# The fourteen middle images written out one by one, in place of a loop with registers

## The reference

```python
# layer 0: attention over rows of each channel
Q, K, V = (_conv1x1(x, W, b).reshape(b * cr, m, n) for W, b in ...)
attn = softmax(einsum('gik,gjk->gij', Q, K), axis=-1)
y = _conv1x1(einsum('gij,gjn->gin', attn, V), Wr, br)
x = batch_norm(y) + x
# layer 1: 8 heads of attention over 1024 tokens, 32 channels a head
q, k, v = split(einsum('oc,bct->bot', w_qkv, group_norm(x)) + b_qkv)
weight = softmax(einsum('bct,bcs->bts', q * scale, k * scale))
x = x + einsum('oc,bct->bot', w_proj, einsum('bts,bcs->bct', weight, v)) + b_proj
# layer 2: linear attention with softmax over channels and over tokens
xn = group_norm(x); k, v = split(conv(xn)); q = softmax(k, axis=1) * q_scale
out = gelu(group_norm(einsum('bde,bdn->ben', einsum('bdn,ben->bde', softmax(k, 2), v), q)))
x = xn + einsum('bchw,oc->bohw', out, out_w) + out_b
# layer 3: 12-tap upsampling by 2 both ways, leaky relu, 12-tap downsampling by 2
x = down(leaky_relu(up(x + bias), 0.2) * sqrt(2))
```

## Time and profile before

| what | value |
|---|---|
| median of 3 runs | 3870.22 us (3865.36 to 3873.83) |
| the profiled execution, its own time | 3865.28 us |
| its span (first to last instruction) | 3863.4 us |
| granted TensorE clock, mean of the span | 0.957 |
| instructions recorded | 72651 |

### The profile page before, as it was taken

One profiled execution on the slowest core, in us unless ns is written; L12 is line 12 of the kernel. 1 busy time (PEld: TensorE's weight loads), 2 busy tenths in 40 slices (PEclk: granted clock), 3 DMA queues, 4 the chain that ended last, 5 costly groups with the idle time before them and its releaser, 6 DMA issues.

```text
span 3863.4 us, 72651 instructions
## 1 busy us (share of the span) xinstructions
PE 3622.2 (94%) x22401; PEld 1790.8 (46%) x22401; DVE 2890.1 (75%) x5019; ACT 2972.7 (77%) x6992; POOL 41.3 (1%) x57
## 2 busy tenths in 40 slices
PE   6989999999999999999999999999999999999987
PEld 3444545354453544545354453544545354453423
DVE  4667778778777777778778787777778778787755
ACT  2888878878787887878878787887878878788852
POOL 0000000000000000000000000000000000000000
PEclk7889999999999999999999999999999999999998
DMA  2212120121211112120121211112120121211100
GB/s 76 58 39 61 40 70 7 51 59 39 72 35 37 45 42 67 40 70 7 50 59 40 72 30 42 45 42 67 40 70 7 51 59 40 72 30 41 34 17 11
DMA packets 75657, 177.20 MB, mean 46 GB/s; under 512 B 16352, under 2 KB 19040, under 8 KB 73184
## 3 DMA queue, kind: packets, MB, share of 16 engines
q1 hardware_dynamic: 74656, 170.38, 16.2%
q10 hardware_dynamic: 576, 1.57, 0.2%
HBM read 36.62 MB, written 17.30 MB: 14 GB/s over the span
## 4 chain that ended last, share of the span: by engine, by line
PE 80%; issue 7%; DVE 7%; ACT 6%; SPq 0%; ACTq 0%; DMA 0%; DVEq 0%; POOL 0%; POOLq 0%
PE ps L1102 29%; PE ps L1167 12%; PE ps L1130 12%; PE ps L1146 10%; PE ps L1718 3%; ACT ps L986 3%; PE ps L1768 2%; DVE mxh L680 2%; PE ps L1653 2%; PE ps L1750 2%; PE ps L1760 2%; PE ps L1665 2%; PE ps L1777 2%; DVE k L819 1%; ACT u L1048 1%
## 5 line engine op out<-in xcount | busy, mean ns | idle before, releaser
L986 ACT ACTIVATE ps<-ps,mxh 128x512 f32<-128x512 f32 x2048 | 1365.8, 674 | 196.3 <-DVE mxh L680 169.2
L680 DVE TENSOR_REDUCE mxh<-ps 128x1 f32<-128x512 f32 x2048 | 1309.9, 679 | 273.9 <-PE ps L1146 266.1
L977 ACT ACTIVATE prob<-ps 128x512 f32<-128x512 f32 x2048 | 1122.0, 611 | 354.2 <-PE ps L1130 347.3
L1130 PE MATMUL ps<-qs,ks 97*128 97x512 f32 x2048 | 892.6, 513 | 38.3 <-issue 29.1
L1146 PE MATMUL ps<-ks,qs 96*128 96x512 f32 x2048 | 703.1, 419 | 33.3 <-ACT ps L986 18.3
L1130 PEld LDWEIGHTS ps<-qs,ks 97*128 97x128 f32 x2048 | 353.9, 195 | 603.9 <-issue 356.2
L1167 PE MATMUL ps<-prob,vo 128*32 128x512 f32 x4096 | 580.2, 640 | 0.0
L1146 PEld LDWEIGHTS ps<-ks,qs 96*128 96x128 f32 x2048 | 404.1, 197 | 179.9 <-ACT ps L986 79.2
L986 ACT ACTIVATION_READ_ACCUMULATOR ps<-ps,mxh 128x1 f32 x2048 | 443.2, 216 | 0.0
L1102 PE MATMUL ps<-xn,wqk 128*128 128x512 f32 x512 | 246.1, 614 | 13.3 <-DVE lo L663 9.3
L1102 PE MATMUL ps<-wkv,xn 128*128 128x512 f32 x512 | 244.5, 607 | 3.7 <-DVE xn L607 3.7
(11 more groups left out here) (121 smaller groups left out, 3576.8 us busy)
## 6 DMA issues: line engine op xcount, KB each, us to landing
qs<-hi SPq DMA_DIRECT2D x256, 128.0 KB, 2.3
ks<-hi SPq DMA_DIRECT2D x248, 128.0 KB, 2.3
xb<-in_x SPq DMA_DIRECT2D x32, 512.0 KB, 4.3
qs<-lo SPq DMA_DIRECT2D x128, 128.0 KB, 2.3
xa<-xb SPq DMA_DIRECT2D x16, 1024.0 KB, 4.6
recs<-recd SPq DMA_DIRECT2D x64, 256.0 KB
out<-xn SPq DMA_DIRECT2D x32, 512.0 KB, 2.6
ks<-lo SPq DMA_DIRECT2D x124, 128.0 KB, 2.3
```

The lines of the kernel that those rows point to most:

```text
L680: dve.tensor_reduce(mxh[:, k, e:e + 1], ps[:, MAX_BANKS[at % 3], :], AX_X, ALU.max, negate=True).then_inc(max_ok.sem, 1)
L977: act.activation(prob[:, n % 2, h, :], ps[:, k % 2, :], ACT.Exp).then_inc(p_ok.sem, 1)
L986: act.activation(ps[:, bank, :], ps[:, bank, :], ACT.Exp, bias=mxh[:, k, e:e + 1], accum_out=sumh[:, m // NT % 2, k, e:e + 1]).then_inc(su ...
L1130: pe.matmul(ps[:, k % 2, :], ks[0:STACK + 1, (u // 2) * Q4 + h, s * P:(s + 1) * P], qs[0:STACK + 1, u, h, :], start=True, stop=True).then_ ...
```

## The change

The loop of images 1 to 14 becomes a Python loop: the same period is written out 14 times, each time with plain numbers for b, i and j. The counter, the copies of the register, the register sums ahead of waits and the 13 jumps back (with the one that falls through) are gone; every wait is for a constant. Images 0 and 15, `first()` and `last()` are as they were. Each engine has the same instructions that work on data, in the same order. The kernel gets some 20 lines shorter, so that a line L1130 of before is L1109 of after.

```diff
     def __call__(self, image, k):
-        image, away = image if isinstance(image, tuple) else (image, 0)
-        return image * (self.per_image * self.size) + ((away * self.per_image + k) * self.size + START)
+        return (image * self.per_image + k) * self.size + START
...
-        def periods(eng, first, period, last):
+        def periods(first, period, last):
 
             first()
             period(0, None, 1)
-            with eng.Fori(1, B - 1) as b:
-                period((b, 0), (b, -1), (b, 1))
-            period(B - 1, B - 2, None)
+            for b in range(1, B):
+                period(b, b - 1, b + 1 if b < B - 1 else None)
             last(B - 1)
-
-        def copied(eng, n, *images):
-
-
-            if n % 4 or not isinstance(images[0], tuple):
-                return images
-            register = eng.alloc_register(f"image_at_step{n}")
-            eng.reg_mov(register, images[0][0])
-            copy = eng.snap(register, min_val=1, max_val=B - 2)
-            return [(copy, away) for _, away in images]
...
             def period(b, i, j):
                 for n in range(STEPS):
-                    b, i, j = copied(pe, n, b, i, j)
                     for pair in range(2):
                         logits(b, n, pair, i)
...
-            periods(pe, first, period, last)
+            periods(first, period, last)
```

More of the change, by code:

```diff
@@ L127, in __call__ @@
     def __call__(self, image, k):
-        image, away = image if isinstance(image, tuple) else (image, 0)
-        return image * (self.per_image * self.size) + ((away * self.per_image + k) * self.size + START)
-def number(image):
-    return image[0] + image[1] if isinstance(image, tuple) else image
+        return (image * self.per_image + k) * self.size + START
 def chain_kernel(nc, x, weights, vectors, rows, filters, consts, recd, out):
@@ L379, in load @@
                 for ct in range(CT):
-                    sp.dma_start(xb[:, ct, :], x[number(j), ct * P:(ct + 1) * P, :]).then_inc(x_in.sem, 16)
+                    sp.dma_start(xb[:, ct, :], x[j, ct * P:(ct + 1) * P, :]).then_inc(x_in.sem, 16)
             def copy_x(b, i, j):
@@ L429, in store @@
                 sp.wait_ge(o3_ok.sem, o3_ok(i, ct + 1))
-                sp.dma_start(out[number(i), ct * P:(ct + 1) * P, :], o3[:, ct, :]).then_inc(stored.sem, 16)
+                sp.dma_start(out[i, ct * P:(ct + 1) * P, :], o3[:, ct, :]).then_inc(stored.sem, 16)
             def side(name, b, i, j):
@@ L464, in period @@
                 for n in range(STEPS):
-                    b, i, j = copied(sp, n, b, i, j)
                     for name in [*beside(2 * n, i, j), *beside(2 * n + 1, i, j)]:
@@ L471, in last @@
                     side(name, None, i, None)
-            periods(sp, first, period, last)
+            periods(first, period, last)
             sp.wait_ge(stored.sem, stored(B, 0))
@@ L505, in period @@
                 for n in range(STEPS):
-                    b, i, j = copied(pool, n, b, i, j)
                     for name in [*beside(2 * n, i, j), *beside(2 * n + 1, i, j)]:
@@ L512, in last @@
                     side(name, None, i, None)
-            periods(pool, first, period, last)
+            periods(first, period, last)
         @block.vector
@@ L936, in period @@
                 for n in range(STEPS):
-                    b, i, j = copied(dve, n, b, i, j)
                     t = turn_at(n)
@@ L958, in last @@
                     side(name, None, i, None)
-            periods(dve, first, period, last)
+            periods(first, period, last)
         @block.scalar
@@ L1073, in period @@
                 for n in range(STEPS):
-                    b, i, j = copied(act, n, b, i, j)
                     for pair in range(2):
@@ L1090, in last @@
                     side(name, None, i, None)
-            periods(act, first, period, last)
+            periods(first, period, last)
         @block.tensor
```

## The result

| | median, us | runs |
|---|---|---|
| before | 3871.27 | 3865.36 to 3873.83 (4) |
| after | 3782.20 | 3780.32 to 3792.89 (4) |

The ratio is 0.9778, with a 95% interval of 0.9756 to 0.9799. The change gains 89 us; the forecast was 44.5, a time of 3824 us with a range from 3806 to 3843. The direction and the jumps came out as forecast. The other half of the gain stands in a term that the prediction had set at 1.4 us.

The account below looks back on a forecast made before the run. PE, busy 94% of the span, was taken as the bound. Jumps 43.1 plus registers 1.4 made 44.5 us less: 3820.8 from the profiled execution, 3825.7 from the median; 3824 us was set between, range 3806 to 3843.

Parts of the forecast that it names:

- The jumps: At the image boundaries: removing 13 jumps gains 43.1 us, about 26 of PE idle time and 17 of half-clock spells.
- The register instructions: Throughout the loop's images, ahead of waits: removing them gains 0.1 us an image, 1.4 us in all.
- the pair that I could measure (0): Line 1115 to line 1155, in the loop and in image 15 with constants: 20.90 us each, no difference.
- Its upper end: Most that removing register instructions could gain: 25 us, if 48 fused operations an image on PE each cost 37 ns.
- register instructions cost more: Rival: in an image's second half they stand between hand-overs of DVE, ACT and PE; up to 25 us, 3800 us; chance 7%.
- the slow clock stays: Rival: at the boundaries the idle time goes but half-clock spells remain; 27 us gained, 3841 us; chance 9%.
- Stalls of new code: Rival: engines stall on written-out instructions not yet fetched; 3925 us if PE is caught twice an image; chance 4%.
- the gap as cover: Rival: PE's 2 us idle at the jump let DVE and ACT catch up, so PE waits later; 3862 us; chance 3%.
- The instruction packets: Instruction fetch: the loop's body is already fetched each turn, 425 packets; written out, fewer register instructions to fetch, costed at nothing.
- The signs named: Profile after: no 3.4 us branch, boundaries 26.9 us at clock 1.00, PE busy some 17 us less, period 228.6 us.

Follow-up runs that it names:

- e1: Against before: the 14 periods written out without jumps, every register instruction kept on all engines; 3819.39 us, ratio 0.9873.
- e5: Against before: loop and registers kept, a prefetch hint added on the loop's back edge; 3826.33 us, ratio 0.9892.
- e9: The kernel after the change, unchanged, in a second round with a second profile; 3785.23 us, ratio 0.9773.
- e6: Against e1: register waits kept on PE alone, constants in the waits of all other engines; 3795.20 us, ratio 0.9808.
- e7: Against e1: constants in PE's waits, register waits kept on all other engines; 3801.44 us, ratio 0.9827.
- e13: Against after: register waits only for DVE at `turn4`, ahead of its copy, plus copies of the image's number; 3803.13 us, ratio 0.9836.
- e12: Against after: constants everywhere, one added DVE maximum over 128 x 160 values ahead of the copy at `turn4`; 3796.58 us, ratio 0.9835.
- e2: Against before: loop and registers kept, two images in the loop's body, so 6 jumps left of 13; 3839.69 us, ratio 0.9925.
- e3: Against before: PE keeps its loop with jumps and registers, the other engines are written out with constants; 3837.89 us, ratio 0.9925.

## Why the prediction was half right

- **The jumps: 43.1 us forecast, 42.9 measured** (419.83 - 376.90 at the boundaries). Its two halves hold too: PE's busy time in these stretches fell by 393.50 - 376.88 = 16.6 us (17 forecast as slow clock), and the rest was idle time. e1 gives 46 us for the jumps alone, e5 41 for the hint. The cut of one stretch at every boundary, with the fall-through as its control, was the right way to read it.
- **The register instructions: this is the step that failed.** The prediction set them at 1.4 us, "the value next to the pair that I could measure (0)", with 25 us as the end. The runs show 34 us (e1 against e9) to 37 (against after's first four runs): 16 at the image's end, 18 in the middle, of which 12 are PE's busy time. The pair that I measured held to the hundredth, 20.90 us, but it is a stretch in which PE is never idle. I said so, named the second half of the image as the place where registers "could stand on the path", and then took the value from the wrong place all the same.
- **Its upper end was too low as well.** 48 instructions of 37 ns an image counted how long they last on PE. The 16 us of the image's end sit on DVE, ahead of a copy that PE waits for, and most of them aren't duration but clock: 0.2 us more of idle time (0.64 for 0.43), and then some 1.5 or 3 us of slower matmuls (10.3 or 11.8 us for the stretch against the 8.8 of one without a spell) in most images.
- **A control was there to read.** The trace of before has `turn4` once with constants, in image 15:

```profile
3740.97 0.28 PE L1155 MATMUL ps<-ident,stat 128*32 128x128 f32 x1 [0.46 <-ACT u L1048]
3741.63 1.13 PE L1760 MATMUL ps<-qe,up_m 64*128 64x512 f32 x4 [0.37 <-DVE srow L712]
```

  The gap behind the transpose is 0.37 us there and 0.64 in the loop, `hu13` takes 1.13 us instead of 2.08 in image 1, and line 1777 starts at 3748.93 (as the same timeline has it), 7.96 us on, against 11.83 in the loop's first turn. Image 15 has no next image to begin, so it is not a clean pair, but it would have spoken against 1.4 us.
- **The rival "register instructions cost more" had 7%.** It named the right mechanism in part (registers between the hand-overs of DVE, ACT and PE) and the right half of the image; its 3800 us was 18 too high, for the reason above.
- **The rival "the slow clock stays"** is wrong at the boundary: clock 1.00 in all 14. Its observation, that the clock falls elsewhere in the image too, was the clue to the rest of the gain; I used it only to argue about the boundary.
- **Stalls of new code, and the gap as cover**: neither is seen. No branch is left, no stretch at a boundary is longer than 26.93 us, the first gap for "issue" in PE's list of waits is at line 1632 and was there before (line 1653). The instruction packets fell with the instructions, as argued.
- **The signs named.** Right: no branch, 1.87 us at the boundary, 26.9 us at clock 1.00, 20.90 us. Wrong: PE's busy time fell by 43 us, not by 17 (16.6 at the boundaries, 128.33 - 106.34 = 22.0 in the end stretches, 9.9 in the middle, and 5.4 of it given back ahead of and behind these stretches), and the period fell to 226.05, not to 228.6.

Open: which register instructions make the 18 us of the middle. e6 and e7 together, 8.3 and 4.6 us over e9, don't add up to them, and neither is far outside the spread of the traces with constants. Open too is why one `turn4` of equal gaps has the spell and the next has not, and why 3 of the 13 jumps of before brought none; those three follow the three images whose end took 11.8 us. The number of spells differs between kernels of nearly equal gaps (8 in e13, 4 in e12), so the count says likelihood and no more.

## What to carry to other kernels

Cut the period into stretches, and read gap, granted clock and busy time for each, in the loop and in the copy outside it: a control from a stretch in which the bottleneck engine is never idle says nothing about stretches in which it waits. Price an instruction not by how long it lasts but by whether it stands behind the last wait of a hand-over to PE; there it counts on any engine, and PE's clock can multiply it. If a loop has to stay, hint its back edge (41 us here for one argument). What would be worth moving in it are the register instructions behind the last wait of a hand-over that PE is idle for; no run here tried to make these values earlier.

## What the runs showed of the hardware

- PE's branch at the loop's end took 3487 ns in the median without a prefetch hint and 357 with it; the least of the 14, where it falls through, took 83 and 88 ns.
- The granted clock answers to small differences of idle time. With mean gaps of 0.87 and 0.64 us at `turn4`, 11 of 14 stretches had a spell at 1.2 GHz; with 0.62 and 0.43, none, and none in a second profile; with a delay by other means (0.62 and 0.66), 4. The gap at the jump (1.92 us at the first) brought one in 10 of 13 cases before, in 6 of 6 in e2 and in 7 of 13 in e3. The Trainium skill, page "TensorE: Matmul & The Clock Gate", section "What's actually happening", has the throttled state as the default, which activity releases. These rows agree in so far as the clock fell behind PE's idle gaps; which state is the default they don't show.
- A copy on DVE that waits for values made of a register got one register instruction for each wait; three of them stood behind the wait for PE and ran some 0.1 us apart. With constants the waits that had long been met were through before PE's transpose had even started.
